# Gate and gate weights of a tile computed one tile ahead of its projections, in a two-layer mixture kernel

## The chip, the core and the metric

The kernel runs on one core of a Trainium2 chip, in one launch. The metric is the device time of one execution in microseconds (us), the median of several runs. The core has a matrix engine (TensorE, PE in the profile; its weight loads are PEld), a vector engine (VectorE, DVE), a scalar engine (ScalarE, ACT), a general engine (GpSimd, POOL) and a queue that here only starts transfers (SyncE, SP). Each engine runs its own instructions strictly in program order and waits on semaphores.

## What is computed

`x` has 16 batches of 512 tokens of 256 values, all in float32. Three residual layers follow each other, the first and the third with the same weights. Cut to what matters:

```
def moe(h):                          # h: layernorm(x); 16 experts of width 64
    logits = unit(h) @ unit_cols(sim) - sigmoid(gates)
    rw = softmax(masked relu(logits))            # gate weights, with a fallback to the top two
    q, k, v = (sum_e rw[:, e] * (h @ W[e]) for W in (q_proj, k_proj, v_proj))
    att = softmax(causal(q @ k.T / 8)) @ v
    return sum_e (att * rw[:, e]) @ o_proj[e]
def top_attention(h):                # 16 heads of width 16
    s = Q @ K.T / 4
    s = where(s < 31st largest of its row, -inf, s)
    return softmax(s) @ V @ Wo.T + bo
x = x + 0.5 * moe(layernorm(x))          # "b" in the kernel
x = x + top_attention(layernorm(x))
x = x + 0.5 * moe(layernorm(x))          # "a" in the kernel
```

## The kernel before

Everything runs on tiles of 128 tokens; a batch has 4 tiles (`TPB`), and there are 64 in all (tiles 0 to 63). The order of work is written out by hand. Each batch owns a span of 64 slots (`SPAN`), a tile 16 (`TILE`). Every engine walks through the same slots, and in a slot it emits the steps that are due there. The table `AT` gives each step's slot relative to its batch, and the step of tile c in the batch comes 16c slots later. `emit` (L246) writes out spans -2 to 1, runs spans 2 to 13 as a hardware loop, and writes out spans 14 to 17 (`FIRST, LOOP, FINAL`).

The middle layer sets the pace of the slots: the 31st largest of each row of scores is found on DVE by seven passes over 512 values (MAX8 at L805, MATCH_REPLACE8 at L807), for 64 units per batch, two of them every second slot from slot 4 on (`TOP`). POOL (L939, L944) and ACT (L710, L715) follow it.

The two mixture layers are jobs "b" and "a", and each tile of a job goes through these steps:

- **Gating.** Load of x (`x_ld`, SP, L304; "a" takes x from the attention layer by `x`, ACT L613, instead), sum, mean, square, rstd (L554, L854, L558, L836), normalised h (L563), its transpose hT (PE L387, ACT L619), logits (PE L393, ACT L624), `shift` (POOL L868), `top`, `pair`, `repl`, `gate` (seven small POOL instructions, L877 to L885), `gate_exp` (ACT L570), `gate_em`, `gate_sum` (ACT L574), `rw` (POOL L893, L895), `rwT` (PE L400, ACT L629), and `rw_st`: an SP transfer (L312) of the 16 x 128 gate weights to DRAM.
- **Scaling and projections.** Four chunks of four experts. SP loads the chunk's gate weights from DRAM, spread over all partitions, into one of two buffers `RB` (L318). POOL multiplies hT by them (`hs`, L903), and PE multiplies the chunk by the expert weights in 16 matmuls into `pQ` (L490). ACT copies q, k and v (`qkv`, L589, L590).
- **Attention and output.** q and k transposed (L406), scores `sc` (L412), row maximum on DVE (L787), `sc_nmax`, `sc_exp`, `sc_rec` (POOL L910, ACT L579, POOL L914), `sc_norm` (L585), `pT` (PE L420), `attT` (PE L426, ACT L650), `mix` (POOL L921, with the gate weights that `rb2` loads, L327), `y` (PE L434, L438, and the residual x at L440), and for "a" the store `out` (SP L332).

Slots per tile of "b", relative to its batch: `x_ld` -115, `x_sum` -112, `gate` -98, `gate_exp` -97, `rw_st` -92, first `RB` load -91, `hs` -88 to -82, `qkv` -80, `sc` -78, `sc_rec` -73, `pT` -70, `mix` -67, `y` -64. For "a": `x` 74, `gate` 87, `rw_st` 93, first `RB` load 93 (after `rw_st` in the same slot), `hs` 96 to 102, `qkv` 104, `sc` 107, `sc_rec` 111, `pT` 114, `mix` 117, `y` 119, `out` 120. The steps after the first `RB` load of one tile therefore alternate with the gating of the next tile: the attention of tile t falls between the gating steps of tile t+1.

On SP all transfers of both jobs stand in one queue. One that must wait (helper `held`, L244) holds back all behind it. At ACT slot 20 of the first span, L689 waits for the output weights `wof` and halves them.

Of the kernel before, what the change touches and what calls it, by code (L numbers as in the profile page):

```python
# [5 lines left out]
F32 = mybir.dt.float32  # L6
ALU = mybir.AluOpType
ACT = mybir.ActivationFunctionType
ds = bass.ds

P = 128
# [25 lines left out]
RINGX = 9  # L37
FIRST, LOOP, FINAL = -2, (2, 13), 17

# [12 lines left out]
    "b": {k: v - SPAN for k, v in {  # L52
        "x_ld": -51, "x_sum": -48, "x_mean": -47, "x_sq": -46, "x_rstd": -45, "h": -44, "hT": -43, "h_rinv": -43,
        "lg": -41, "shift": -40, "top": -39, "pair": -38, "repl": -37, "gate": -34, "gate_exp": -33,
# [3 lines left out]
    }.items()},  # L58
}

PROJ = {"Q0": 57 - SPAN, "K0": 59 - SPAN, "V0": 61 - SPAN, "V1": 62 - SPAN, "Q1": 68 - SPAN, "K1": 70 - SPAN}
# [59 lines left out]
def build(nc, x, wqk, bqk, wv, bv, wo, bo, sim, gates, wf, wof, out):  # L121
    with ExitStack() as ctx:
# [58 lines left out]
        class Job:  # L181

            def __init__(self, n):
                self.n = n
                self.at = AT[n]
                self.x = sb(f"x_{n}", P, TPB, D)
                self.h = sb(f"h_{n}", P, D)
                self.junk = sb(f"junk_{n}", P, D)
                self.hT = sb(f"hT_{n}", P, 2, KC * P)
                self.Lr, self.L, self.R, self.fb, self.fb2, self.pos, self.mk, self.RL, self.eg, self.em, self.rw = (  # L190
# [14 lines left out]
                self.attT = sb(f"attT_{n}", P, P)  # L205
                self.rows = nc.dram_tensor(f"rows_{n}", (2, E, P), F32, kind="Internal").ap()
                self.F = bank(f"pF{n}")
# [6 lines left out]
        jobs["a"].sem.update({k: sem(k) for k in ("ctx_rec", "ctx_norm", "out_st")})  # L214
        jobs["b"].sem.update({k: sem(k) for k in ("y_mean", "y_sq", "y_eps", "y_rstd", "y_bias", "xn_norm")})

# [54 lines left out]
        def _(sp):  # L271
# [25 lines left out]
            def ffn(J, w, j):  # L297
                q = J.sem
                if at := tile(J, "x_ld", w, j):
                    t, c = at  # L300
                    if not (isinstance(t, int) and t < TPB):
                        held(sp, q["read"], fill("b", w, j + J.at["y"] - J.at["x_ld"] - SPAN) + 1)
                    held(sp, q["x_in"], t * 16)
                    sp.dma_start(J.x[:, c % TPB, :], x_t[ds(t, 1)].rearrange("a p d -> (a p) d")).then_inc(q["x_in"], 16)  # L304
                    if isinstance(t, int) and t == 0:
                        early_loads()
                if at := tile(J, "rw_st", w, j):
                    t, c = at
                    held(sp, q["read"], fill(J.n, w, j + J.at["rwT"] - J.at["rw_st"]) + 1)
                    if not (isinstance(t, int) and t < 2):  # L310
                        held(sp, s_mix, earlier(w, j + J.at["mix"] - J.at["rw_st"] - 2 * TILE, MIXES.values()) + 1)
                    sp.dma_start(J.rows[c % 2], J.rwT[:]).then_inc(q["rw_st"], 16)  # L312
                for k in range(4):
                    if at := tile(J, "hs", w, j, 3 - 2 * k):
                        t, c = at
                        held(sp, q["rw_st"], 16 * t + 16)
                        held(sp, s_hs, chunk_no(w, j + 3) - 1)
                        sp.dma_start(RB[:, k % 2, :, :].rearrange("p e t -> p (e t)"),  # L318
                                     J.rows[c % 2, 4 * k:4 * k + 4, :].rearrange("e t -> (e t)").partition_broadcast(P)
                                     ).then_inc(s_rb[k % 2], 16)  # L320
                if at := tile(J, "rb2", w, j):
                    t, c = at
                    held(sp, q["rw_st"], 16 * t + 16)
                    held(sp, s_mix, earlier(w, j, MIXES.values()))
                    pairs = J.rows[c % 2].rearrange("(c o) t -> o c t", o=2)
                    for o in range(2):
                        sp.dma_start(RB2[o * ED:(o + 1) * ED, :, :], pairs[o].partition_broadcast(ED)  # L327
                                     ).then_inc(s_rb2, 16)
                if at := tile(J, "out", w, j):
                    t, c = at  # L330
                    held(sp, q["read"], fill("a", w, j + J.at["y"] - J.at["out"]) + 1)
                    sp.dma_start(out_t[ds(t, 1)].rearrange("a p d -> (a p) d"), y[:]).then_inc(q["out_st"], 16)  # L332
# [10 lines left out]
        def _(pe):  # L343
# [17 lines left out]
            def ffn(J, w, j):  # L361
# [27 lines left out]
                if at := tile(J, "lg", w, j):  # L389
                    t, c = at  # L390
                    wait(pe, q["read"], n)
                    for k in range(KC):
                        mm = nc.tensor.matmul(F[:, 0:E], J.hT[:, c % 2, k * P:(k + 1) * P], simn[:, k, :],  # L393
                                              start=k == 0, stop=k == KC - 1)
# [40 lines left out]
                if at := tile(J, "y", w, j):  # L435
                    t, c = at
                    for k in range(4, 8):
                        mm = nc.tensor.matmul(F[:, 0:D], mixT[:, k, :], wof_sb[:, k, :], start=False, stop=False)  # L438
                    mm.then_inc(s_yd, 1)
                    nc.tensor.matmul(F[:, 0:D], ident[:], J.x[:, c % TPB, :], start=False, stop=True  # L440
                                     ).then_inc(q["full"], 1)
# [101 lines left out]
        def _(act):  # L543
# [5 lines left out]
            def ffn(J, w, j):  # L549
                q, F = J.sem, J.F  # L550
                if J.n == "b" and (at := tile(J, "x_sum", w, j)):
                    t, c = at
                    act.wait_ge(q["x_in"], 16 * t + 16)
                    nc.scalar.activation(J.junk[:], J.x[:, c % TPB, :], ACT.Copy, accum_out=J.sm[:]).then_inc(q["x_sum"], 1)  # L554
                if at := tile(J, "x_sq", w, j):
                    t, c = at
                    act.wait_ge(q["x_mean"], t + 1)
                    nc.scalar.activation(J.junk[:], J.x[:, c % TPB, :], ACT.Square, bias=J.mn[:], accum_out=J.vs[:]  # L558
                                         ).then_inc(q["x_sq"], 1)
                if at := tile(J, "h", w, j):  # L560
                    t, c = at
                    act.wait_ge(q["x_bias"], t + 1)
                    nc.scalar.activation(J.h[:], J.x[:, c % TPB, :], ACT.Identity, scale=J.rstd[:], bias=J.nmr[:]  # L563
                                         ).then_inc(q["h_norm"], 1)
# [38 lines left out]
            def leave(J, w, j):  # L603
# [6 lines left out]
                if at := tile(J, "x", w, j):  # L610
                    t, c = at
                    act.wait_ge(q["full"], n)
                    nc.scalar.activation(J.x[:, c % TPB, :], F[:, 0:D], ACT.Copy, accum_out=J.sm[:]).then_inc(q["read"], 1)  # L613
                if at := tile(J, "hT", w, j):
                    t, c = at
                    if not (isinstance(t, int) and t < 2):
                        act.wait_ge(s_hs, chunk_no(w, j + J.at["hs"] + 6 - J.at["hT"] - 2 * TILE) + 1)
                    act.wait_ge(q["full"], n)
                    nc.scalar.copy(J.hT[:, c % 2, :], F[:, 0:D]).then_inc(q["read"], 1)  # L619
                if at := tile(J, "lg", w, j):  # L620
# [195 lines left out]
        def _(pool):  # L816
# [21 lines left out]
            def ffn(J, w, j):  # L838
# [57 lines left out]
                for k in range(4):  # L896
                    if at := tile(J, "hs", w, j, -2 * k):
# [6 lines left out]
                            HS[:, k % 2, :, :, :],  # L904
                            J.hT[:, c % 2, :].rearrange("p (k t) -> p k t", k=KC).unsqueeze(1).broadcast_to([P, 4, KC, P]),
                            RB[:, k % 2, :, :].unsqueeze(2).broadcast_to([P, 4, KC, P]), ALU.mult).then_inc(s_hs, 1)
# [86 lines left out]
```

## Time and profile before

| what | value |
|---|---|
| median of 3 runs | 4994.49 us (4994.19 to 5000.2) |
| profiled execution, device time | 4995.95 us |
| its span, first to last instruction | 4994.1 us |
| busy: DVE / PE / POOL / ACT | 91% / 80% / 74% / 68% of the span |
| granted TensorE clock, mean | 0.922 |
| DRAM traffic | 215 MB read, 9.4 MB written |

The span is the profiled execution alone; its device time is 1.85 us longer, and that is 1.5 us above the median. In a timeline row the first number is the start in us from the span's beginning, the second the duration, then engine, line, operation, result and inputs; in brackets the idle time of the engine before it and what ended it. A row of busy time by stage gives the stretch, its length, the busy time of PE, PEld, DVE, ACT and POOL with the number of instructions of each, the granted TensorE clock, the share of the transfer engines, and GB/s. A granted clock of 1.00 is TensorE's 2.4 GHz, 0.50 is 1.2 GHz.

### The profile page before, as it was taken

What the parts mean: (1) busy time and instruction counts of PE and PEld (TensorE: products, weight loads), DVE (VectorE), ACT (ScalarE), POOL (GpSimd) and SP (SyncE); (2) the same over time, 40 slices, a digit from 0 to 9 for tenths busy, and PEclk for the clock granted to TensorE, in tenths of its full rate; (3) what the DMA queues carried; (4) which work ended last, traced back from release to release, by engine and by line L of the source; (5) the groups of instructions that cost most, each with busy time, mean ns of one, the idle gap of its engine ahead of it and who ended that gap; (6) DMA issues with size and microseconds to landing.
All of it is one profiled execution on the core that took longest, in us unless ns stands there. A gap on an engine that the chain in (4) does not pass through costs nothing.

```text
span 4994.1 us, 112055 instructions
## 1 busy us (share of the span) xinstructions
PE 3991.0 (80%) x29004; PEld 3263.9 (65%) x29004; DVE 4551.9 (91%) x10838; ACT 3382.4 (68%) x8245; POOL 3717.9 (74%) x5070
## 2 busy tenths in 40 slices
PE   5666688888888888888888888788888888877666
PEld 4555567676676667666667667666766677655555
DVE  0299999999999999999999999999999999999940
ACT  2366667777777777777777777777777777766641
POOL 4555678888888888887878787878888888755554
PEclk8888899999999999999999999999999999988787
DMA  2210111111111111111111111111111111110011
GB/s 82 50 29 20 31 46 49 50 49 51 48 52 48 52 47 52 48 50 48 52 47 52 48 52 48 52 48 52 47 52 48 51 49 51 46 29 26 23 41 48
DMA packets 243193, 232.29 MB, mean 47 GB/s; under 512 B 27075, under 2 KB 176580, under 8 KB 242244
## 3 DMA queue, kind: packets, MB, share of 16 engines
q1 hardware_dynamic: 242500, 224.49, 16.5%
q8 instruction: 260, 4.26, 0.3%
q14 instruction: 433, 3.55, 0.2%
HBM read 214.98 MB, written 9.44 MB: 45 GB/s over the span
## 4 chain that ended last, share of the span: by engine, by line
issue 42%; POOL 24%; DVE 15%; PE 14%; ACT 2%; DVEq 2%; POOLq 1%; SPq 1%; ACTq 0%; DMA 0%
POOL HS L903 10%; DVE M L805 9%; PE pQ L490 5%; DVE W L807 5%; POOL S L944 4%; POOL mixT L921 3%; DVEq L240 2%; PE pFa L434 1%; PE pFa L438 1%; PE pFb L458 1%; PE pST L474 1%; PE pST L507 1%; PE pFa L378 1%; PE pFa L380 0%; PE pFa L379 0%
## 5 line engine op out<-in xcount | busy, mean ns | idle before, releaser
L490 PE MATMUL pQ<-wf_sb,HS 128*128 128x192 f32 x8192 | 1622.7, 357 | 559.2 <-POOL HS L903 558.9
L805 DVE MAX8 M<-W 128x8 f32<-128x512 f32 x3072 | 1965.4, 683 | 0.0
L490 PEld LDWEIGHTS pQ<-wf_sb,HS 128*128 128x128 f32 x8192 | 1487.5, 209 | 645.6 <-POOL HS L903 505.9
L807 DVE MATCH_REPLACE8 W<-M,W 128x512 f32<-128x512 f32 x2048 | 1371.1, 678 | 0.0
L944 POOL TENSOR_TENSOR S<-S,RL 128x512 f32<-128x512 f32 x1024 | 1307.9, 1278 | 2.2 <-issue 2.0
L710 ACT ACTIVATE RL<-S,NBI 128x512 f32<-128x512 f32 x1024 | 760.4, 743 | 418.1 <-POOL S L944 417.4
L939 POOL TENSOR_TENSOR NBI<-M,edge 128x4 f32<-128x4 f32 x512 | 102.6, 200 | 909.7 <-DVE M L805 882.1
L715 ACT ACTIVATE S<-S,NBI 128x512 f32<-128x512 f32 x1024 | 746.3, 729 | 2.1 <-POOL S L944 2.1
L807 DVE MATCH_REPLACE8 W<-M,S 128x512 f32<-128x512 f32 x1024 | 685.5, 678 | 0.0
L805 DVE MAX8 M<-S 128x8 f32<-128x512 f32 x1024 | 652.6, 680 | 29.2 <-issue 28.4
L699 ACT COPY S<-pST 128x512 f32<-128x512 f32 x1024 | 524.6, 597 | 185.2 <-PE pST L474 185.2
L903 POOL TENSOR_TENSOR HS<-hT_b,RB 128x1024 f32<-128x1024 f32 x256 | 605.7, 2366 | 22.0 <-DMA RB<-rows_b 12.1
L903 POOL TENSOR_TENSOR HS<-hT_a,RB 128x1024 f32<-128x1024 f32 x256 | 606.4, 2369 | 19.5 <-DMA RB<-rows_a 11.8
L705 ACT COPY PTs<-pST 128x512 f32<-128x512 f32 x1024 | 527.4, 607 | 19.3 <-PE pST L507 16.6
L507 PE MATMUL pST<-ident,S 128*128 128x128 f32 x4096 | 509.4, 279 | 11.3 <-ACT S L699 11.3
L507 PEld LDWEIGHTS pST<-ident,S 128*128 128x128 f32 x4096 | 477.1, 146 | 29.3 <-ACT S L699 13.6
L533 PEld LDWEIGHTS pO<-PTs,V 128*32 128x32 f32 x8192 | 214.8, 112 | 216.2 <-issue 184.0
L474 PE MATMUL pST<-KT,QT 32*128 32x512 f32 x2048 | 308.6, 673 | 11.7 <-ACT PTs L705 11.7
L533 PE MATMUL pO<-PTs,V 128*32 128x128 f32 x8192 | 286.6, 282 | 10.6 <-ACT ctxr L725 10.6
L434 PE MATMUL pFa<-wof_sb,mixT 128*128 128x256 f32 x512 | 139.5, 420 | 110.5 <-POOL mixT L921 110.5
L434 PEld LDWEIGHTS pFa<-wof_sb,mixT 128*128 128x128 f32 x512 | 98.8, 203 | 140.0 <-issue 103.1
L807 DVE MATCH_VALUE_LOAD W<-M,W 128x8 f32 x2048 | 163.0, 80 | 0.0
(220 smaller groups left out, 5403.5 us busy)
## 6 DMA issues: line engine op xcount, KB each, us to landing
RB<-rows_b SPq DMA_DIRECT2D x384, 256.0 KB, 3.3
RB<-rows_a SPq DMA_DIRECT2D x384, 256.0 KB, 3.3
x_b<-in_x SPq DMA_DIRECT2D x64, 128.0 KB, 2.9
out_y<-y SPq DMA_DIRECT2D x64, 128.0 KB, 1.7
wf_sb<-in_wf SPq DMA_DIRECT2D x1, 3072.0 KB, 10.4
wof_sb<-in_wof SPq DMA_DIRECT2D x1, 1024.0 KB, 12.4
rows_b<-rwT_b SPq DMA_DIRECT2D x64, 8.0 KB, 1.3
rows_a<-rwT_a SPq DMA_DIRECT2D x64, 8.0 KB, 1.3
```

The lines of the kernel that those rows point to most:

```text
L474: nc.tensor.matmul(pST[h][:], QT[r:r + 32, g // 2, g % 2, m * P:(m + 1) * P], KT[r:r + 32, g // 2, :], start=True, stop=True).then_inc(s_s ...
L490: mm = nc.tensor.matmul(pQ[:, 0:QKV], HS[:, k % 2, e, i, :], wf_sb[:, i, at:at + QKV], start=k + e + i == 0, stop=(k, e, i) == (3, 3, 1))
L507: mm = nc.tensor.transpose(pST[h][:, k * P:(k + 1) * P], S[:, (4 * c + h) % RING, k * P:(k + 1) * P], ident[:])
L533: mm = nc.tensor.matmul(pO[32 * h:32 * h + 32, 0:P], V[:, k, HG * g + h, :], PTs[:, h, k * P:(k + 1) * P], start=k == 0, stop=k == TPB - 1)
L699: nc.scalar.copy(S[:, (4 * c + h) % RING, :], pST[h][:]).then_inc(s_ev, 1)
L705: nc.scalar.copy(PTs[:, h, :], pST[h][:]).then_inc(s_pe, 1)
L710: nc.scalar.activation(RL[:, c % 2, :], S[:, c % RING, :], ACT.Relu, bias=NBI[:, c % RING, 1:2], scale=-STEEP).then_inc(s_rl, 1)
L715: nc.scalar.activation(S[:, c % RING, :], S[:, c % RING, :], ACT.Exp, bias=NBI[:, c % RING, 0:1], scale=HD ** -0.5).then_inc(s_ex, 1)
L805: nc.vector.max(m, src[i]).then_inc(s_tk, 1)
L807: nc.vector.match_replace(W[:, i, :], m, src[i], -BIG).then_inc(s_tk, 1)
L903: nc.gpsimd.tensor_tensor(HS[:, k % 2, :, :, :], J.hT[:, c % 2, :].rearrange("p (k t) -> p k t", k=KC).unsqueeze(1).broadcast_to([P, 4, KC ...
L944: nc.gpsimd.tensor_tensor(S[:, c % RING, :], S[:, c % RING, :], RL[:, c % 2, :], ALU.subtract).then_inc(s_sub, 1)
```

## The change

The gating steps of each tile move one tile (16 slots) ahead of its scaling, projections and attention. For "b" the gating keys (`GATING`) are set 16 slots earlier. For "a", whose input comes from the attention layer, the gating stays and all that follows it comes 16 slots later, its output too. The first span becomes -3, and the loop runs over spans 3 to 12 instead of 2 to 13, so two more spans are written out. hT gets four buffers instead of two, the DRAM rows of gate weights four instead of two. "b" uses its four x buffers as two for gating and two for the residual: x is loaded from DRAM a second time (`x_again`, 128 KB per tile, 6 slots before `y`), and PE waits for it at L440. No arithmetic instruction is added or taken away.

```diff
-FIRST, LOOP, FINAL = -2, (2, 13), 17
+FIRST, LOOP, FINAL = -3, (3, 12), 17
...
+GATING = ("x_ld", "x_sum", "x_mean", "x_sq", "x_rstd", "h", "hT", "h_rinv", "lg", "shift", "top", "pair", "repl", "gate",
+          "gate_exp", "gate_em", "gate_sum", "rw", "rwT", "rw_st")
+AT["b"] = {k: v - TILE * (k in GATING) for k, v in AT["b"].items()}
+AT["a"] = {k: v + TILE * (k not in GATING + ("ctx_rec", "ctx_norm", "ctxT", "x")) for k, v in AT["a"].items()}
...
+                self.new = (lambda c: c % TPB) if n == "a" else (lambda c: c % 2)
+                self.old = (lambda c: c % TPB) if n == "a" else (lambda c: 2 + c % 2)
...
-                self.hT = sb(f"hT_{n}", P, 2, KC * P)
+                self.hT = sb(f"hT_{n}", P, TPB, KC * P)
...
-                self.rows = nc.dram_tensor(f"rows_{n}", (2, E, P), F32, kind="Internal").ap()
+                self.rows = nc.dram_tensor(f"rows_{n}", (TPB, E, P), F32, kind="Internal").ap()
...
                 if at := tile(J, "x_ld", w, j):
                     t, c = at
-                    if not (isinstance(t, int) and t < TPB):
-                        held(sp, q["read"], fill("b", w, j + J.at["y"] - J.at["x_ld"] - SPAN) + 1)
+                    if not (isinstance(t, int) and t < 2):
+                        held(sp, q["h_norm"], t - 1)
                     held(sp, q["x_in"], t * 16)
-                    sp.dma_start(J.x[:, c % TPB, :], x_t[ds(t, 1)].rearrange("a p d -> (a p) d")).then_inc(q["x_in"], 16)
+                    sp.dma_start(J.x[:, c % 2, :], x_t[ds(t, 1)].rearrange("a p d -> (a p) d")).then_inc(q["x_in"], 16)
...
+                if at := tile(J, "x_again", w, j):
+                    t, c = at
+                    if not (isinstance(t, int) and t < 2):
+                        held(sp, q["read"], fill("b", w, j + J.at["y"] - J.at["x_again"] - 2 * TILE) + 1)
+                    held(sp, q["x_again"], 16 * t)
+                    sp.dma_start(J.x[:, 2 + c % 2, :], x_t[ds(t, 1)].rearrange("a p d -> (a p) d")
+                                 ).then_inc(q["x_again"], 16)
...
-                    if not (isinstance(t, int) and t < 2):
-                        held(sp, s_mix, earlier(w, j + J.at["mix"] - J.at["rw_st"] - 2 * TILE, MIXES.values()) + 1)
-                    sp.dma_start(J.rows[c % 2], J.rwT[:]).then_inc(q["rw_st"], 16)
+                    if not (isinstance(t, int) and t < TPB):
+                        held(sp, s_mix, earlier(w, j + J.at["mix"] - J.at["rw_st"] - SPAN, MIXES.values()) + 1)
+                    sp.dma_start(J.rows[c % TPB], J.rwT[:]).then_inc(q["rw_st"], 16)
...
-                    nc.tensor.matmul(F[:, 0:D], ident[:], J.x[:, c % TPB, :], start=False, stop=True
+                    if J.n == "b":
+                        pe.wait_ge(q["x_again"], 16 * t + 16)
+                    nc.tensor.matmul(F[:, 0:D], ident[:], J.x[:, J.old(c), :], start=False, stop=True
```

## Rows read from the trace of the kernel before

**Rows 1.** The page: busy time of the engines; loads of x, to landing.

```profile
PE 3991.0 (80%) x29004; PEld 3263.9 (65%) x29004; DVE 4551.9 (91%) x10838; ACT 3382.4 (68%) x8245; POOL 3717.9 (74%) x5070
x_b<-in_x SPq DMA_DIRECT2D x64, 128.0 KB, 2.9
```

**Rows 2.** Busy time by stage: head, first spans, loop part, tail.

```profile
0.00:227.40 227.40, 141.95 (x644) 116.84 (x644) 8.92 (x49) 56.19 (x189) 118.71 (x200) 0.86 0.25 68
227.40:794.00 566.60, 407.05 (x2846) 323.74 (x2847) 566.53 (x1335) 380.30 (x887) 364.31 (x503) 0.83 0.12 33
794.00:4222.00 3428.00, 2882.40 (x21720) 2370.53 (x21718) 3399.63 (x8091) 2520.20 (x6168) 2776.50 (x3782) 0.96 0.18 50
4793.70:4994.10 200.40, 144.04 (x765) 122.29 (x765) 5.88 (x24) 46.39 (x149) 102.37 (x132) 0.82 0.18 47
```

**Rows 3.** Waits of DVE from 230 to 4790 us: total, times, longest.

```profile
DVE M L805 <- issue: 28.4, 11, 2.9
```

**Rows 4.** Timeline, SP in the tail: stores of the output, first and last.

```profile
4807.02 0.34 SPq L332 DMA_DIRECT2D out_y<-y  x1
...
4939.41 0.34 SPq L332 DMA_DIRECT2D out_y<-y  x1
4969.68 0.34 SPq L332 DMA_DIRECT2D out_y<-y  x1
4992.03 0.34 SPq L332 DMA_DIRECT2D out_y<-y  x1
```

**Rows 5.** Timeline, tail: first chunks on POOL, weights stored and loaded.

```profile
4888.99 2.34 POOL L903 TENSOR_TENSOR HS<-hT_a,RB 128x1024 f32<-128x1024 f32 x1 [1.20 <-DMA RB<-rows_a]
...
4945.69 0.32 SPq L312 DMA_DIRECT2D rows_a<-rwT_a  x1
4946.69 0.58 POOL L914 TENSOR_TENSOR rrs_a<-rs_a,minus_one 128x1 f32<-128x1 f32 x1 [0.82 <-ACT Sr_a L579]
4947.19 0.33 SPq L318 DMA_DIRECT2D RB<-rows_a  x1
4947.70 1.26 SPq L327 DMA_DIRECT2D RB<-rows_a  x2
...
4950.55 2.34 POOL L903 TENSOR_TENSOR HS<-hT_a,RB 128x1024 f32<-128x1024 f32 x1 [3.28 <-DMA RB<-rows_a]
```

**Rows 6.** Timeline, head: first chunk of tiles 0, 2 and 3 on POOL.

```profile
37.27 2.34 POOL L903 TENSOR_TENSOR HS<-hT_b,RB 128x1024 f32<-128x1024 f32 x1 [0.56 <-DMA RB<-rows_b]
...
100.33 2.34 POOL L903 TENSOR_TENSOR HS<-hT_b,RB 128x1024 f32<-128x1024 f32 x1 [1.90 <-DMA RB<-rows_b]
...
132.63 2.34 POOL L903 TENSOR_TENSOR HS<-hT_b,RB 128x1024 f32<-128x1024 f32 x1 [0.74 <-DMA RB<-rows_b]
```

**Rows 7.** Timeline, start: the gate chains of tiles 0 and 1.

```profile
15.08 1.91 ACT L689 ACTIVATE wof_sb<-wof_sb 128x2048 f32<-128x2048 f32 x1 [7.01 <-DMA wof_sb<-in_wof]
...
20.23 0.22 POOL L868 TENSOR_TENSOR L_b<-Lr_b,sig 128x16 f32<-128x16 f32 x1 [1.16 <-ACT Lr_b L624]
...
23.72 0.31 ACT L570 ACTIVATE eg_b<-RL_b,nv_b 128x16 f32<-128x16 f32 x1 [3.57 <-POOL mk_b L885]
...
27.39 0.35 SPq L304 DMA_DIRECT2D x_b<-in_x  x1
...
29.63 0.42 ACT L554 ACTIVATE junk_b<-x_b 128x256 f32<-128x256 f32 x1 [5.60 <-DMA x_b<-in_x]
...
36.49 0.23 POOL L868 TENSOR_TENSOR L_b<-Lr_b,sig 128x16 f32<-128x16 f32 x1 [1.15 <-ACT Lr_b L624]
```

**Rows 8.** Busy time and granted clock around the first chunk of tile 3.

```profile
127.00:131.00 4.00, 1.80 (x7) 1.24 (x7) 0.55 (x1) 3.21 (x11) 2.26 (x7) 0.68 0.10 34
131.00:135.00 4.00, 0.81 (x3) 0.30 (x3) 0.18 (x1) 1.24 (x4) 3.13 (x4) 0.50 0.96 210
```

**Rows 9.** Timeline, PE in the tail: a first chunk of 16 matmuls, the second.

```profile
4825.60 4.30 PE L490 MATMUL pQ<-wf_sb,HS 128*128 128x192 f32 x16 [2.34 <-POOL HS L903]
4830.06 2.77 PE L490 MATMUL pQ<-wf_sb,HS 128*128 128x192 f32 x16
```

## Prediction before the run

> **What bounds the kernel now.** I read the page first: DVE is busy 91% of the span, POOL and ACT about 70% [rows 1]. Next the busy time by stage. There are three stages with different limits [rows 2]. In the head, 0 to 227.4 us, DVE has next to nothing to do: 8.9 us. From 227.4 on it is full: 566.53 of 566.60 us in the written-out spans ahead of the loop, and 3399.6 of 3428 us in the part that holds the loop. From 4793.7 to the end, 200.4 us, it works 5.9 us. The waits of DVE between 230 and 4790 us are a single line: 11 waits of "issue", 28.4 us in total, 2.6 us each [rows 3]. A loop of 12 passes has 11 back edges, and the written-out spans show none. So the middle is DVE's work plus the back edges, and no change in the order of the mixture layers can shorten it. What can move is the head, the tail and the number of back edges.
>
> In head and tail one job alone goes from tile to tile, and it is bound by latency. The stores of the output in the tail are 30 to 34 us apart, seven of them from 4807.0 to 4992.0, 185.0 us in all; the last two intervals are 30.3 and 22.4 us [rows 4].
>
> **The steady part: 0 but for the loop.** The table keeps the place of every step within the 16 slots of a tile, since the shift is exactly one tile. In every engine's program the same kinds of instructions follow each other as before, with another tile's data. DVE has the same work. The waits of the gating on DVE keep their place in its program. I cost this at 0. Two back edges fall away: 2 x 2.6 = **-5.2 us** [rows 3]. The two further written-out spans cost what the present ones do, 0.07 us of idle in 566.6 [rows 2].
>
> The Trainium skill ("Runtime: NRT & Kernel Launch", Instruction fetch mechanics) says that sequential code is streamed ahead and that a taken branch forces a fetch before execution goes on; by that rule too each removed pass saves one stall, and the 2.6 us are this trace's own.
>
> `x_again` adds one transfer per tile on SP. It is issued after the third `RB` load, which waits for the first chunk on POOL; behind it stands the fourth `RB` load, which waits for the second chunk. Its own conditions were met a tile earlier, so it holds the queue for about 0.35 us, the issue of such a load [rows 7]. It lands 2.9 us later [rows 1], six slots before `y` needs it. 0; if it came late, PE at L440 would wait, and behind it the projections of the other job. I bound this at 0 to +1 us per tile of the head.
>
> **The tail: one more period.** In the last batch the gating of "a" stays where it is and the rest comes 16 slots later, so after DVE's end the same slots see the tiles 56 to 62 where they saw 57 to 63, and tile 63 still has to follow. That is one more interval. Which interval? Gating still ends at the same slot, so the one added contains no gating at all: scaling and projections of tile 63 beside the attention of tile 62. The nearest row is the present last but one interval, 30.27 us. In it POOL finished `sc_rec` at 4947.27 and then stood 3.28 us until the `RB` load landed, because the gate weights of that tile had been stored only at 4945.69 [rows 5]. In the new interval no `rw_st` stands ahead of the load in SP's queue and the weights are long in DRAM; only the buffer must be free. So it starts at once: 30.27 - 3.28 = **+27.0 us**. The ends: 22.4 us, the last interval, which has no chunks, and 30.3 us.
>
> **What the earlier gating gives back.** The wait that the change can remove is that of the first chunk (L903) for its `RB` load. It doesn't vanish in the other intervals. `rw_st` of the next tile now stands directly ahead of this tile's first `RB` load in SP's queue, and it waits for `rwT` at the same place as before. What goes is the wait for the store's completion: store at 4945.69, load at 4947.19, and back to back issues are 0.51 us apart, as the next pair shows [rows 5]. The load comes 1.50 - 0.51 = 1.0 us earlier, and the gain is the smaller of that and the wait. In the tail there are four such waits, 1.07, 1.20, 0.81 and 3.28 us; the second and the last are shown [rows 5]. So 1.0 + 1.0 + 0.8 + 1.0 = **-3.8 us**. In the head there are five, of tiles 1 to 5, 1.67, 1.90, 0.74, 0.67 and 1.09 us; tiles 2 and 3 are shown [rows 6]. There the loads can come 1.0, 1.6, 1.0, 1.0 and 1.4 us earlier (the store took longer at two of them): 1.0 + 1.6 + 0.7 + 0.7 + 1.1 = **-5.1 us**. The second chunk waits too, but the third waits for PE's first chunk, which ends later. If none of this came, 0; if every wait went wholly, -12.4.
>
> What else could shorten an interval does not: the small POOL instructions of gating, y's mean and rstd, and the row maximum's scale stay in the same order, only the gating ones are those of the tile after. No interval of the head loses its gating.
>
> **The head: a second gating first.** The first chunk of tile 0 follows the gating of tile 1 up to slot -92 and that of tile 2 up to `shift` in slot -88, where today it follows tile 1's `shift`. From `shift` to the start of `gate_exp` tile 0 took 20.23 to 23.72, 3.49 us; `gate_exp` takes 0.31 us, and the next tile's `x_sum` follows it on ACT; from `x_sum` to `shift` tile 1 took 29.63 to 36.49, 6.86 us [rows 7]. So the `shift` of tile 2 comes at 36.49 + 3.49 + 0.31 + 6.86 = 47.15, and after its 0.23 us the first chunk at 47.4 instead of 37.27 [rows 6]: **+10.1 us**. Its `RB` load, behind the store of tile 1 near 43.2, lands by about 47. What lies ahead of that is hidden: the halving of `wof` (L689) now stands before ACT's first work instead of after it and delays tile 0, whose `h` followed it at 16.9 us anyway, by some 3 us; the gating of tile 0 then waited until x of tile 1 arrived at 29.6, held by the early loads until 27.39 [rows 7]. The chain would have to slip more than 5 us to show. Bounds: +6.9 (one pass from `x_sum` to `shift`) to +13.
>
> **Sum.** Head +10.1 - 5.1; tail +27.0 - 3.8; loop -5.2: together +23.0 us, 0.46%. On the span 4994.1 to 5017.1 us; the device time is 1.85 us above the span and the median 1.5 us below the profiled execution, and the change carries over to it as it is: 4994.5 + 23.0 = **5017.5 us**.
>
> **Rivals.**
> *A, the clock stays up (not slower).* Around a first chunk the granted clock is 0.50 and PE needs 4.3 to 5.5 us for 16 matmuls, where a later chunk needs 2.77 us [rows 8, 9]. A shorter wait of POOL might keep the clock at 1.00. Price: 1.5 to 2.7 us each, at four tiles of the head and five of the tail, some 20 us, plus 2.7 in the added interval: 5017.5 - 23 = 4995. It decides only if the clock falls during the removed 1 us. Against it: the clock is at 0.68 on average from 127 to 131 us and at 0.50 from 131 on, before the first chunk of tile 3 starts at 132.63 [rows 6, 8]; and a first chunk with no wait for a transfer and PE idle for only 2.34 us took 4.30 us all the same [rows 9]. 7%.
> The Trainium skill ("TensorE: Matmul & The Clock Gate", Why this matters for your kernels) says that it is idle gaps between bursts of matmuls that drop the clock; by that rule a shorter gap speaks for A.
> *B, the waits stay.* The `RB` load stays tied to the store ahead of it, or lands later because store and load now meet: nothing given back, the added interval 30.3 us. 10.1 + 30.3 - 5.2 = +35: 5030 us. 15%.
> *C, DVE starves.* The doubled load of x or the later steps of "a" hold SP's queue and DVE waits in the steady part; 1 us per batch gives +16 more: 5034 us. For it: the one queue serves both jobs. Against it: no wait but the back edges today [rows 3]. 6%.
> *D, the head is hidden.* If the first chunk of tile 0 were held today by something else that ends late, the +10 would not come: 5007 us. Against: POOL goes on 0.56 us after its last gating step [rows 6]. 10%.
>
> **The numbers.** The forecast itself 62% (5010 to 5025). Range for 8 in 10: 5006 to 5031; it takes in D and B. Some 0.2% (10 us) is what a measurement of this kernel can tell from no change. Slower by more: the forecast, B, C and most of D, 0.89. Within: A's middle and the low end of D, 0.08. Faster: 0.03, if A comes with faster attention matmuls.
>
> **What would show it.** Nine back edge waits of DVE instead of 11. DVE's first MAX8 at L805 near 232 us instead of 227.5. Its last near 4793 + 5 - 5, that is, within 2 us of today's. Eight output stores after it instead of seven, the last but one interval near 27 us with no wait for `RB`. First chunk waits in head and tail down by about 1 us. I am wrong if DVE shows new waits in the middle, if PE's first chunks take 2.8 us, or if the added interval is above 30 or below 25 us.

## The result and the profile after

| | before | changed |
|---|---|---|
| median | 4997.16 us (4994.19 to 5000.2, 6 runs) | 5016.81 us (5013.17 to 5021.32, 6 runs) |
| ratio | | 1.0039, 95% interval 1.0027 to 1.0052 |
| span of the profiled execution | 4994.1 us | 5014.8 us |
| head, until DVE's first MAX8 of 512 values | 227.5 us | 230.3 us |
| middle, until DVE's last MAX8 of 512 values has ended | 4565.4 us | 4558.8 us |
| tail, from there on | 201.3 us | 225.8 us |

The change costs 19.7 us, 0.39%. The three stages of the two traces account for 20.7 us: head +2.8, middle -6.6, tail +24.5.

The lines of after have numbers 7 to 16 higher: the chunk on POOL is L919 instead of L903, the projections on PE L506 instead of L490, MAX8 L821 instead of L805, the loads of the spread weights (`RB`) L332 instead of L318, the store of the gate weights L326 instead of L312.

Busy time by stage, after (columns as in [rows 2]); the last row is the tail:

```profile
0.00:230.20 230.20, 141.26 (x651) 115.57 (x651) 9.34 (x52) 59.79 (x202) 123.57 (x218) 0.88 0.26 70
230.20:794.00 563.80, 394.54 (x2744) 310.63 (x2745) 563.72 (x1328) 376.89 (x875) 348.98 (x494) 0.82 0.12 32
794.00:4222.00 3428.00, 2885.93 (x21735) 2386.87 (x21734) 3405.26 (x8104) 2525.01 (x6171) 2777.53 (x3787) 0.96 0.19 51
4789.10:5014.80 225.70, 164.96 (x862) 141.27 (x860) 6.31 (x26) 50.33 (x161) 115.45 (x140) 0.83 0.19 50
```

DVE is as full in the middle as it was. Its only waits there are again the jumps back to the start of the loop (the back edges), nine now in place of eleven [rows 3]:

```profile
DVE M L821 <- issue: 22.7, 9, 2.8
```

The stores of the output in the tail, after: eight, where [rows 4] has the first and the last of seven.

```profile
4803.22 0.34 SPq L346 DMA_DIRECT2D out_y<-y  x1
...
4934.07 0.34 SPq L346 DMA_DIRECT2D out_y<-y  x1
4962.30 0.34 SPq L346 DMA_DIRECT2D out_y<-y  x1
4989.48 0.34 SPq L346 DMA_DIRECT2D out_y<-y  x1
5011.96 0.34 SPq L346 DMA_DIRECT2D out_y<-y  x1
```

From first to last store it is 208.7 us instead of 185.0, +23.7. The last two intervals are 27.2 and 22.5 us. The one of 27.2 is new: the one after the last gating. The one ahead of it takes 28.2 us, where its counterpart took 30.3 [rows 4].

The timeline of POOL and SP shows why. These are the last three tiles' first chunks, with what stands around them:

```profile
4911.52 0.32 SPq L326 DMA_DIRECT2D rows_a<-rwT_a  x1
4912.02 0.32 SPq L332 DMA_DIRECT2D RB<-rows_a  x1
...
4915.26 2.34 POOL L919 TENSOR_TENSOR HS<-hT_a,RB 128x1024 f32<-128x1024 f32 x1 [0.23 <-DMA RB<-rows_a]
...
4939.93 0.32 SPq L326 DMA_DIRECT2D rows_a<-rwT_a  x1
4940.44 0.33 SPq L332 DMA_DIRECT2D RB<-rows_a  x1
...
4943.73 2.34 POOL L919 TENSOR_TENSOR HS<-hT_a,RB 128x1024 f32<-128x1024 f32 x1 [2.35 <-DMA RB<-rows_a]
...
4962.83 0.32 SPq L332 DMA_DIRECT2D RB<-rows_a  x1
...
4969.59 0.57 POOL L930 TENSOR_TENSOR rrs_a<-rs_a,minus_one 128x1 f32<-128x1 f32 x1 [0.82 <-ACT Sr_a L595]
4970.12 4.64 POOL L919 TENSOR_TENSOR HS<-hT_a,RB 128x1024 f32<-128x1024 f32 x2
```

Store and load are now 0.5 us apart instead of 1.5 [rows 5], and the wait of the chunk is 0.23 and 2.35 us where its counterparts waited 0.81 and 3.28. The load is still tied to the store ahead of it in the queue. Only for tile 63 no store stands there: the load is issued at 4962.83, and the chunk follows `sc_rec` at once.

In the head, the first chunk of tile 0 starts at 46.75 us instead of 37.27 [rows 6], behind a second gating:

```profile
36.04 0.22 POOL L884 TENSOR_TENSOR L_b<-Lr_b,sig 128x16 f32<-128x16 f32 x1 [1.16 <-ACT Lr_b L640]
...
46.58 0.22 POOL L884 TENSOR_TENSOR L_b<-Lr_b,sig 128x16 f32<-128x16 f32 x1 [1.16 <-ACT Lr_b L640]
46.75 2.34 POOL L919 TENSOR_TENSOR HS<-hT_b,RB 128x1024 f32<-128x1024 f32 x1
...
71.49 2.34 POOL L919 TENSOR_TENSOR HS<-hT_b,RB 128x1024 f32<-128x1024 f32 x1 [0.51 <-DMA RB<-rows_b]
104.04 2.34 POOL L919 TENSOR_TENSOR HS<-hT_b,RB 128x1024 f32<-128x1024 f32 x1
```

From `shift` to `shift` (L884) it is 10.5 us. Five tiles later DVE starts only 2.8 us late. Of the 6.7 us given back, 4.8 lie between the first chunks of the tiles 1 and 2 (32.6 us instead of 37.3); the part on the clock takes them apart.

### The profile page after: what moved, and what is told of

It reads as the page before. It is cut to its first block, busy times and chain, and to the rows that moved or that the text cites. A ratio compares the mean times of both kernels' runs of the same rounds, so it can differ in the third digit from the quotient of the medians.

```text
span 5014.8 us, 110179 instructions
## 1 busy us (share of the span) xinstructions
PE 3996.5 (80%) x29004; PEld 3280.2 (65%) x29004; DVE 4551.7 (91%) x10838; ACT 3385.7 (68%) x8245; POOL 3712.4 (74%) x5070
## 4 chain that ended last, share of the span: by engine, by line
issue 44%; POOL 22%; DVE 16%; PE 13%; ACT 2%; DVEq 2%; POOLq 1%; SPq 1%; DMA 0%; ACTq 0%
DVE M L821 10%; POOL HS L919 9%; DVE W L823 5%; PE pQ L506 5%; POOL S L960 4%; POOL mixT L937 3%; DVEq L247 1%; PE pFa L448 1%; PE pFa L452 1%; PE pFb L474 1%; PE pST L490 1%; PE pST L523 1%; PE pFa L392 1%; PE pFa L394 0%; PE pFa L393 0%
## 5 line engine op out<-in xcount | busy, mean ns | idle before, releaser
L506 PE MATMUL pQ<-wf_sb,HS 128*128 128x192 f32 x8192 | 1648.3, 361 | 563.5 <-POOL HS L919 563.4
L821 DVE MAX8 M<-W 128x8 f32<-128x512 f32 x3072 | 1957.7, 677 | 0.0
L506 PEld LDWEIGHTS pQ<-wf_sb,HS 128*128 128x128 f32 x8192 | 1514.3, 212 | 650.5 <-POOL HS L919 497.3
L821 DVE MAX8 M<-S 128x8 f32<-128x512 f32 x1024 | 650.1, 675 | 23.6 <-issue 22.7
L919 POOL TENSOR_TENSOR HS<-hT_a,RB 128x1024 f32<-128x1024 f32 x256 | 606.1, 2368 | 19.8 <-PE pQ L506 11.3
L919 POOL TENSOR_TENSOR HS<-hT_b,RB 128x1024 f32<-128x1024 f32 x256 | 605.3, 2364 | 16.2 <-PE pQ L506 11.0
L490 PE MATMUL pST<-KT,QT 32*128 32x512 f32 x2048 | 306.1, 668 | 15.5 <-ACT PTs L721 15.5
L803 DVE TENSOR_REDUCE mxr_a<-Sr_a 128x1 f32<-128x128 f32 (+1 forms) x64 | 29.9, 467 | 155.9 <-ACT Sr_a L656 155.9
## 6 DMA issues: line engine op xcount, KB each, us to landing
wf_sb<-in_wf SPq DMA_DIRECT2D x1, 3072.0 KB, 10.1
```

Of the source, the lines that this page charges most:

```text
L490: nc.tensor.matmul(pST[h][:], QT[r:r + 32, g // 2, g % 2, m * P:(m + 1) * P], KT[r:r + 32, g // 2, :], start=True, stop=True).then_inc(s_s ...
L506: mm = nc.tensor.matmul(pQ[:, 0:QKV], HS[:, k % 2, e, i, :], wf_sb[:, i, at:at + QKV], start=k + e + i == 0, stop=(k, e, i) == (3, 3, 1))
L821: nc.vector.max(m, src[i]).then_inc(s_tk, 1)
L919: nc.gpsimd.tensor_tensor(HS[:, k % 2, :, :, :], J.hT[:, c % TPB, :].rearrange("p (k t) -> p k t", k=KC).unsqueeze(1).broadcast_to([P, 4, ...
```

## The experiments

Each kernel was compared with the kernel before on the same chip, five rounds; the medians of before in these comparisons lie between 4998.3 and 4999.6 us, and one comparison can tell differences of about 0.1%.

**One layer alone.** The change touches both layers by two lines of the table. Leaving out one of them undoes it for that layer. First the changed kernel without the line for a:

```diff
-AT["a"] = {k: v + TILE * (k not in GATING + ("ctx_rec", "ctx_norm", "ctxT", "x")) for k, v in AT["a"].items()}
```

> The change for layer b alone: the gating of b runs a tile ahead, layer a keeps its slots, spans and loop are those of the changed kernel. Theory (head and tail are separate costs, the tail is a's alone): against the kernel before, DVE starts some 3 us later (230.3 against 227.5 us in the traces), the middle is 6 us shorter (two back edges of 2.6 us, and half of the under 1 us of DVE work that moved out of it), the tail from DVE's last MAX8 is the 201.4 us of before: together -3 us, 4994 us. Rival (the cost comes from b as much as from a, through the doubled load of x or SP's queue): +7 us or more.

Measured: 4997.22 us, ratio 0.9996 (0.9987 to 1.0005). Head 230.2, middle 4561.4, tail 202.0 us: DVE starts late, the middle is shorter, though by 4.0 us and not by 6, and the tail is the old one. The span is 4993.5 us. The rival's +7 us lies outside the interval: b's doubled load costs nothing that can be seen.

Now layer a alone, again as an edit of the changed kernel:

```diff
-FIRST, LOOP, FINAL = -3, (3, 12), 17
+FIRST, LOOP, FINAL = -2, (3, 12), 17
...
-AT["b"] = {k: v - TILE * (k in GATING) for k, v in AT["b"].items()}
```

> The change for layer a alone, with the loop over spans 3 to 12; b keeps its gating in its old slots (it still loads x a second time). Theory: the head is the one of before (DVE starts at 227.5 us), the middle is 6 us shorter, the tail has one more interval and is 24 us longer: +18 us, 5015 us. It should hold nearly the whole difference of the changed kernel. Rival (the head costs as much as the tail): +10 us.

Measured: 5013.07 us, ratio 1.0031 (1.0019 to 1.0043). Tail 225.9 us, eight stores, the last intervals 28.5, 27.0 and 22.4 us. That is the tail of the changed kernel. The times alone don't decide here: +13.5 us on the medians lies between theory (+18) and rival (+10), and the interval holds both. The stages do. The tail is 24.6 us longer than before, DVE starts at 225.4 us, no later than in the kernel before. So nearly the whole loss is layer a's one additional interval behind DVE's end.

**The loop alone.** This is an edit of the kernel before.

```diff
-FIRST, LOOP, FINAL = -2, (2, 13), 17
+FIRST, LOOP, FINAL = -2, (3, 12), 17
```

> The kernel before with spans 2 and 13 written out, so that the loop has 10 passes instead of 12; nothing else differs. Theory (each back edge stalls DVE 2.6 us, and written-out spans stall nothing): 9 waits of DVE called issue instead of 11, -5.2 us, 4992 us. Rival (written-out code costs as much elsewhere): 0.

Measured: 4993.97 us, ratio 0.9990 (0.9981 to 0.9999). DVE's waits for MAX8 in the whole of this kernel:

```profile
DVE M L805 <- issue: 22.7, 9, 2.8
```

and the timeline's first MAX8 of 512 values:

```profile
230.41 1.29 DVE L805 MAX8 M<-S 128x8 f32<-128x512 f32 x2 [0.84 <-ACT S L699]
```

The interval just leaves out the rival's 0. The middle is 4559.8 us, 5.6 shorter, and DVE's waits went from 28.4 to 22.7 us, for two back edges. But the row of the timeline was not expected. The head of this kernel is the same code as in the kernel before, and yet DVE starts at 230.4 us instead of 227.5; the span, 4994.0 us, is hardly shorter. An execution of the same head can differ by 3 us, as much as the difference read between before and after. One pair of traces doesn't measure the head. All traces with either order of the gating of b together do it better, those of the experiments below included:

| | DVE's start, us, each kernel's trace | mean |
|---|---|---|
| b's gating as before (6 traces) | 227.5, 230.4, 225.4, 224.5, 228.3, 228.1 | 227.35 |
| b's gating a tile ahead (6 traces) | 230.3, 231.4, 230.2, 230.9, 230.5, 231.1 | 230.72 |
| | tail, us | mean |
| a as before (7 traces) | 201.3, 203.8, 202.0, 204.6, 205.8, 204.9, 203.8 | 203.7 |
| a's later steps a tile later (4 traces) | 225.8, 225.9, 228.5, 227.6 | 226.9 |

(The two kernels with spare matmuls are left out, and from the tail the kernel that reorders SP's queue, whose tail is 224.4 us.) Head +3.4, tail +23.2, middle -5.6 by the loop: +21.0 us, against 19.7 measured.

**What is left of the wait.** In the changed kernel, the load of a tile's first weights was put ahead of the store of the next tile's in SP's queue.

```diff
-        "gate_em": -32, "gate_sum": -31, "rw": -30, "rwT": -29, "rw_st": -28, "hs": -24, "qkv": -16, "qkT": -15,
+        "gate_em": -32, "gate_sum": -31, "rw": -30, "rwT": -29, "rw_st": -26, "hs": -24, "qkv": -16, "qkT": -15,
```

With it, in SP's queue of both layers, the block of the `RB` loads stands ahead of the block of `rw_st`.

> The changed kernel with one order turned around on SP: the first load of the spread gate weights of a tile is issued ahead of the store of the next tile's gate weights, for both layers. Theory (what is left of the first chunks' waits comes from that store standing ahead in the queue): the waits of the first chunks for their load, 0.5 and 0.2 us in the head and 0.2, 0.2 and 2.35 us in the tail, go to 0; -3 us against the changed kernel, nearly all of it in the tail interval whose gating is ending. Rival (the loads are bound by the transfer engines, not by the queue): 0.

Measured: 5016.47 us, ratio 1.0034 (1.0021 to 1.0046). The mechanism is as expected: no first chunk waits for its load any more, in head or tail. The gain is not to be seen in the median: the ratio of the changed kernel was 1.0039, and the two intervals hold both the theory's -3 us and the rival's 0. The waits of the chunks in the tail, first of the changed kernel, then of this one:

```profile
POOL HS L919 <- PE pQ L506: 11.3, 6, 3.4
POOL HS L919 <- DMA RB<-rows_a: 8.5, 8, 2.4
```

```profile
POOL HS L919 <- PE pQ L506: 13.2, 6, 3.1
POOL HS L919 <- DMA RB<-rows_a: 3.2, 2, 2.9
```

The wait for the load fell by 5.3 us and the wait of the third chunk for PE rose by 1.9. In the interval that had the longest wait the chunk starts at once, but now the second chunk waits, since its load stands behind the store:

```profile
4942.00 0.32 SPq L334 DMA_DIRECT2D rows_a<-rwT_a  x1
...
4943.41 2.35 POOL L919 TENSOR_TENSOR HS<-hT_a,RB 128x1024 f32<-128x1024 f32 x1
4948.69 2.35 POOL L919 TENSOR_TENSOR HS<-hT_a,RB 128x1024 f32<-128x1024 f32 x1 [2.93 <-DMA RB<-rows_a]
4951.51 2.35 POOL L919 TENSOR_TENSOR HS<-hT_a,RB 128x1024 f32<-128x1024 f32 x1 [0.47 <-PE pQ L506]
```

That interval went from 28.2 to 26.3 us. The next went from 27.2 to 25.8 although nothing in it was changed: there the first chunk's matmuls took 4.22 instead of 5.46 us.

```profile
4972.60 5.46 PE L506 MATMUL pQ<-wf_sb,HS 128*128 128x192 f32 x16 [5.48 <-POOL HS L919]
```

```profile
4972.78 4.22 PE L506 MATMUL pQ<-wf_sb,HS 128*128 128x192 f32 x16 [5.49 <-POOL HS L919]
```

The last interval took 23.4 us instead of 22.5, and the first of the tail 35.0 instead of 33.6. The whole tail, 224.4 us, is the shortest of all with eight stores (the others: 225.8 to 228.5), but one trace doesn't tell the theory's 3 us from that spread.

**The clock.** The same changed kernel, then one with spare matmuls:

> The changed kernel once more, unaltered, so that the other kernels of this comparison stand beside it on the same chip. Both theories: +20 us against the kernel before. The start of DVE and the single intervals of the tail should come out within 1 us of the first trace if they depend on the program alone, and up to 3 us apart if they also depend on where TensorE's clock happens to rise and fall in an execution.

Measured: 5021.29 us, ratio 1.0045 (1.0031 to 1.0059). DVE starts at 231.4 us; the tail's intervals are 34.9, 32.2, 33.5, 33.0, 28.5, 27.0 and 22.4 us, where the first trace had 33.6, 33.0, 32.5, 31.8, 28.2, 27.2 and 22.5. One program's intervals differ by up to 1.3 us between these executions, in both directions. (Between the two traces of the short loop kernel below it is up to 1.9 us, and DVE starts at 224.5 and at 228.3 us.)

In the next kernel `keep_warm(cols, count)` issues that many matmuls whose result nobody reads, and `quiet` limits them to the spans ahead of DVE's work and the last span:

```diff
+                    for key in ("qkT", "sc", "rwT", "hT"):
+                        if quiet(w, j) and tile(J, key, w, j):
+                            keep_warm(256, 1)
...
+                        if k == 0 and quiet(w, j) and not (isinstance(t, int) and t == 0):
+                            keep_warm(512, 3)
                         pe.wait_ge(s_hs, chunk_no(w, j))
```

> The changed kernel with spare matmuls whose result nobody reads, only in the spans ahead of DVE's work and in the last span: one of 256 columns after each transpose or score step of gating and attention, three of 512 columns while TensorE waits for a tile's first chunk. Theory (what is left of the differences between executions and between tiles is the clock: a first chunk takes 4.2 to 5.5 us at the low clock and 2.8 us at the high one): first chunks take about 2.8 us, the third chunk waits less for TensorE, and head and tail lose 1 to 2 us per tile, -10 us in all, unless the spare matmuls stand in the way. Rival (the clock does not hang on this work): the first chunks stay at 4.2 to 5.5 us and the time rises by the spare matmuls, +5 us or so.

Measured: 5024.53 us, ratio 1.0048 (1.0034 to 1.0062), not to be told from the unaltered kernel by its time. Its DVE starts at 237.6 us, though, outside all that the order has shown without spare matmuls (230.2 to 231.4). Two pieces of PE's timeline, of the tiles 2 and 3:

```profile
104.80 2.74 PE L491 MATMUL pST<-wf_sb,ident 128*128 128x512 f32 x6
108.28 2.87 PE L515 MATMUL pQ<-wf_sb,HS 128*128 128x192 f32 x16 [0.74 <-POOL HS L932]
...
135.52 5.33 PE L491 MATMUL pST<-wf_sb,ident 128*128 128x512 f32 x6
140.64 2.81 PE L515 MATMUL pQ<-wf_sb,HS 128*128 128x192 f32 x16
```

The first chunks of tiles 2 and 3 took 2.9 and 2.8 us instead of 5.0 and 4.7. But at tile 3 the three spare matmuls themselves met the low clock: 5.33 us instead of 2.74, and the chunk, ready at 137.8, had to wait for them until 140.6. And the clock fell elsewhere: the fourth chunk of tile 3 took 4.55 us. At tile 5 the first chunk took 2.8 us without help too; there the spare matmuls stood in front of it for 3.72 us, and from POOL's start on the chunk to PE's it took 7.8 us instead of 4.3. In the tail the three first chunks behind spare matmuls took 3.07, 5.49 and 2.87 us; ahead of the one of 5.49, PE had stood idle for 3.63 us after the spare ones. With the chunk of 2.87 us, the added interval took 24.3 us instead of 27.0. So a first chunk's length is the clock's, as the theory says, but the theory's gain of 10 us did not come. The expectation was wrong in that it counted the gain at the chunks, and not the low stretch, which only moved ahead of them, nor the time of the spare matmuls where the clock was up anyway.

The clock also tells apart the heads of the old order. The fourth chunk of tile 1 on PE, and the granted clock around it, before and after:

```profile
80.68 4.51 PE L490 MATMUL pQ<-wf_sb,HS 128*128 128x192 f32 x16 [2.17 <-POOL HS L903]
```

```profile
80.00:84.00 4.00, 3.32 (x10) 3.32 (x11) 0.00 (x0) 0.00 (x0) 0.81 (x2) 0.58 0.00 0
```

```profile
88.13 2.87 PE L506 MATMUL pQ<-wf_sb,HS 128*128 128x192 f32 x16 [2.17 <-POOL HS L919]
```

```profile
88.00:91.00 3.00, 2.87 (x17) 2.87 (x18) 0.00 (x0) 0.00 (x0) 0.26 (x2) 1.00 0.00 0
```

In the trace of before, PE was at 0.58 there, mostly its low level, and the chunk took 4.5 us; in that of after it was at 1.00 and took 2.87 us. From the first chunk of tile 1 to that of tile 2 it is 37.3 and 37.6 us in two traces of the old order, the two with such a long fourth chunk, 33.8 to 34.8 us in the four others, and 32.6 to 33.0 us in all six of the new one. The fourth chunk of tile 2 is long (4.5 us) in three traces of the old order and in none of the new. Together:

| long fourth chunks at the tiles 1 and 2, b's gating as before | DVE's start, us |
|---|---|
| none (2 traces) | 224.5, 225.4 |
| one (3 traces) | 227.5, 228.1, 228.3 |
| two (1 trace) | 230.4 |

So the 3 us between two executions of the same head go with such a stretch at the low clock: the kernel before had one, the loop experiment two. Against the executions that had none, the new order, which had none in six traces, starts DVE 5.8 us later, not 3.4. That the new order keeps the clock up there is what the traces show; why it does, no experiment tells. PE stood idle for 2.17 us ahead of the chunk in both rows. (At tile 4 the fourth chunk is long in traces of both orders, and DVE's start hardly follows it.)

**No loop.** If back edges are worth 2.6 us, there is more to take.

```diff
-FIRST, LOOP, FINAL = -2, (2, 13), 17
+FIRST, LOOP, FINAL = -2, (7, 8), 17
```

> The kernel before with a loop over spans 7 and 8 only, all others written out. Theory: one wait of DVE called issue instead of 11, 10 x 2.6 us less: 4971 us. Rival (longer written-out code stalls by itself): less than 10 us.

Measured: 4973.27 us, ratio 0.9950 (0.9937 to 0.9964), 25.7 us less for ten back edges. And again in the last comparison:

> The kernel before with a loop over spans 7 and 8 only, once more, as the measure for the next three. Both theories: -26 us against the kernel before.

Measured: 4975.47 us, 0.9952 (0.9939 to 0.9966). With the spare matmuls:

> The same long written-out kernel before, with the spare matmuls in head and last span as well. Theory: the gains add up, 26 us from the back edges and 5 to 10 us from head and tail: 4963 us. Rival: the spare matmuls bring nothing here, 4971 us.

Measured: 4973.13 us, 0.9946 (0.9932 to 0.9959), nothing more: the theory's further 5 to 10 us did not come. DVE starts at 234.5 us, 6 to 10 us later than in the two traces without spare matmuls; the tail is 202.0 us against 204.6 and 205.8. DVE's waits in the middle of the first of these kernels:

```profile
DVE M L805 <- issue: 2.9, 1, 2.9
DVE crec L774 <- ACT ctxr L725: 0.5, 1, 0.5
```

The last step takes the loop out of the kernel before altogether:

```diff
-FIRST, LOOP, FINAL = -2, (2, 13), 17
+FIRST, LOOP, FINAL = -2, (8, 7), 17
...
-            with eng.Fori(LOOP[0], LOOP[1] + 1) as i:
-                for j in range(SPAN):
-                    slot(Window(i, *LOOP), j)
```

> The kernel before with every span written out and no loop at all. Theory (each back edge is worth 2.6 us and nothing else is): no wait of DVE called issue, -2.6 us against the short loop kernel, 4970 us. Rival (waits against constants in place of registers also save time on the queues of the engines that head and tail hang on): more than that.

Measured: 4972.71 us, 0.9948 (0.9935 to 0.9962). No wait called issue is left, the middle is 4538.0 us against 4539.6; these last 1.6 us are less than the comparison can tell. Against the 2.9 us of the last back edge stand 1.2 us more of waits for ACT, 1.7 us in place of 0.5:

```profile
DVE crec L771 <- ACT ctxr L722: 1.7, 3, 0.6
```

This and the short loop beat both kernels. Next, the changed kernel with the short loop:

> The changed kernel with the same short loop over spans 7 and 8, so that the change stands without its side effect on the loop. Theory (the change costs head and tail +26 us and the two back edges hid 5.5 us of it): +25 us against the kernel before with the short loop, as a ratio 1.005, and within 2 us of the kernel before itself. Rival (the middle gains something else too): less than +20 us against the short loop kernel.

Measured: 4997.40 us, ratio 0.9999 to the kernel before (0.9990 to 1.0008), and 21.9 us above the short loop kernel of the same comparison. That is between theory (+25) and rival (under +20). Its stages: head 230.5, middle 4538.2, tail 227.6, against 228.3, 4539.6 and 205.8: +2.2, -1.4 and +21.8. The middle gains at most 1.4 us beyond the loop. Last, the same with b's gating a tile ahead and layer a as before:

> The gating a tile ahead for layer b alone, with the short loop. Theory (the head is 2 to 3 us later, the rest as before): +2 us against the short loop kernel of before, 4975 us. Rival (b's earlier gating gains in the head): -2 us.

Measured: 4977.30 us, 0.9961 (0.9948 to 0.9975), 1.8 us above the short loop kernel. The forecast of +2 fits, but the difference is inside the noise, and the rival's -2 can't be excluded by the time; the means of the heads above say +3.4.

## Why the prediction was right, point by point

Forecast 5017.5 us, measured 5016.8, both on medians; +23.0 us forecast over the runs then known, +19.7 measured over all. That the two times agree to 0.7 us is luck: the median of before came out 2.7 us higher with more runs, and the change itself was 3.3 us smaller than forecast. The mechanism held, a cost at each end and two back edges less in the middle, but its steps did not hold equally well.

- **The tail, +27.0 for the added interval.** Measured 27.2, 27.0 and 27.0 us (after, its repetition, a alone), and 25.8 us in two more traces (SP's queue reordered, short loop), in which the first chunk took 4.2 and 4.3 us on PE instead of 5.5, and after which the last interval took 1 us more. The step that named the last but one interval without its 3.28 us as the nearest row held, for a first chunk as slow as in that row (5.42 us). The run with layer a alone shows that a brings it.
- **The tail, -3.8 given back.** Measured -3.3 in the first trace (+23.7 less 27.0), and +23.2 for the tail over all traces. That the load would stay tied to the store held to the tenth: 0.5 us apart. The sum was better than its parts: counted were 1.0, 1.0, 0.8 and 1.0 us, and those four intervals of the first trace gave 0.9, 0, 0.1 and 2.1. The earlier load is not fully worth its microsecond, since the third chunk waits for PE, whose first chunk takes 4.2 to 5.5 us by the clock.
- **The loop, -5.2.** Measured -5.6 (the loop alone). The term of the sum was 0.4 too small. Some 0.9 us more can be DVE work of one gating and one attention tile that moved out of the middle: DVE is busy 9.3 us in the head instead of 8.9 and 6.3 in the tail instead of 5.9. I had cost the middle at 0 beside the loop. The runs do not settle it: against kernels before with the same loop, the middle is 1.4 us shorter with the short loop, and with the loop over spans 3 to 12 between 1.0 us shorter (the first trace) and 1.6 us longer (b alone).
- **The head, +10.1.** Measured +9.5: one pass of gating is 10.5 us from `shift` to `shift`. The displaced halving of `wof` stayed hidden: the second `shift` came at 36.04 us instead of 36.49 [rows 7].
- **The head, -5.1 given back.** The trace says -6.7; the means over six traces each say 3.4 - 9.5 = -6.1. The term came out too small, and its parts were wrong. Against the two executions of the old order without a long fourth chunk only 3.7 us of the 9.5 came back (5.8 are left), less than the 5.1 counted; the other 2.4 us of the mean go with the clock, which the sum did not have. At tile 5 I counted 1.1 us, and nothing was left of it at DVE's start: PE did the projections of the middle layer (L474) until 203.5 us, and the third chunk, which had not waited for PE in the trace of before, waited 1.4 us. From that chunk to DVE's start the trace has 31.0 us instead of 29.7. At tile 2 I counted 1.6 us, and 4.8 came in this pair of traces, some 1.6 of it because the clock stayed up in the fourth chunk of tile 1 and 1.0 because it rose earlier in the first (4.22 us instead of 5.24).
- **Rival A, the clock stays up.** I gave the clock no part in the forecast. At the first chunks that was right: 4.2 to 5.5 us after, too. At the fourth chunks of the tiles 1 and 2, which the forecast did not consider, it did stay up, and the 2.4 us above go with it: a small part of the rival was at work in the head. Spare matmuls on PE brought the first chunks of the tiles 1 to 4 to 2.8 to 2.9 us. The Trainium skill ("TensorE: Matmul & The Clock Gate", Why this matters for your kernels) has it that the clock drops in idle gaps between bursts of matmuls. These traces agree with it, though the same 2.17 us of idle time ahead of a chunk went with either level. The rule alone gave no gain here, since the low stretch has to be spent on something that nobody waits for.
- **B, C, D.** Waits fell, DVE did not starve, the head's delay showed in the first chunk. None of the three happened.
- **The signs named.** Nine back edges, eight stores and the shorter waits came as named. Two were off: DVE's first MAX8 came at 230.3 us and not near 232, and its last ended 3.8 us earlier than before (4789.0 us instead of 4792.8), where at most 2 us were named, since the head came out 2.2 us and the middle 1.4 us shorter than counted.

## What to carry to other kernels

This kernel is a software pipeline: the steps of several tiles overlap, and one engine sets the pace in the middle. Moving a step a tile ahead gained next to nothing there and cost at both ends, where the pace setter has no work: one more interval at the end (27 us), one more pass of the moved steps at the start (9.5 us). It gives back only the waits that end last there; look for what stands ahead of the awaited transfer in its own queue. A few us of difference in such a stage can be the clock of one execution: here one program's head varied by 3.8 us, so take several traces. A hardware loop of few long passes can cost more than it seems: here writing it out was worth 25 us, more than the change moved.

## What was not expected of the hardware

Executions of one program differed by 3 us and more in the head (224.5 to 230.4 us in six traces with the same steps of gating), and the intervals of the tail by up to 1.3 us, by where TensorE's clock rose and fell; the middle, which is DVE's, repeated within 0.3 us where the program was the same (4539.5 and 4539.6). A second trace of the same program is needed before a difference of 3 us in such a stage is explained.
